# The out projection of an attention and mixture-of-experts kernel in three fp32r passes, with the low part of its input made on VectorE

## What is computed

```python
q1, k1, v1 = heads(ln(x) @ Wq1), heads(ln(x) @ Wk1), heads(ln(x) @ Wv1)
q2, k2, v2 = heads(ctx @ Wq2), heads(ctx @ Wk2), heads(ctx @ Wv2)
out1 = softmax(q2 @ k1.T * SCALE) @ v1
out2 = softmax(q1 @ k2.T * SCALE) @ v2
out = merge_heads(out1 * alpha + out2 * (1 - alpha))        # 256 x 512 for a sequence
x = x + out @ Wout + bout                                   # the out projection
h = ln(x)
scores = renormalised top 4 of softmax(h @ gate_w.T)
x = x + sum over experts of scores * (silu(h @ w1) * (h @ w3)) @ w2
```

## Time and profile before

| | us |
|---|---|
| median of 3 runs | 2166.13 |
| lowest, highest | 2165.26, 2168.65 |
| the profiled execution | 2171.79 |
| its span, first to last instruction | 2170.0 |

### The profile page before, as it was taken

One profiled execution on the slowest core, in us unless ns is written; L12 is line 12 of the kernel. 1 busy time (PEld: TensorE's weight loads), 2 busy tenths in 40 slices (PEclk: granted clock), 3 DMA queues, 4 the chain that ended last, 5 costly groups with the idle time before them and its releaser, 6 DMA issues.

```text
span 2170.0 us, 51710 instructions
## 1 busy us (share of the span) xinstructions
PE 1921.2 (89%) x15782; PEld 1684.2 (78%) x15783; DVE 1387.6 (64%) x3231; ACT 1235.5 (57%) x3605; POOL 1224.9 (56%) x1688
## 2 busy tenths in 40 slices
PE   6899999999999999999999999996898888888500
PEld 5788888888888888888888888885888888888500
DVE  4567666766667666677666776678554444444398
ACT  5666666666666666667666676663444444444300
POOL 3356666566665656666666666665455454554400
PEclk9999999999999999999999999998999999998855
DMA  4331111111111111101111101116664444444299
GB/s 131 114 96 44 44 46 61 39 44 42 48 61 39 44 40 50 51 34 39 39 42 51 39 34 44 39 61 188 192 215 143 143 143 140 140 143 139 109 412 360
DMA packets 158560, 210.80 MB, mean 97 GB/s; under 512 B 24224, under 2 KB 131376, under 8 KB 158512
## 3 DMA queue, kind: packets, MB, share of 16 engines
q1 hardware_dynamic: 123696, 129.95, 19.0%
q0 software_dynamic: 26112, 71.86, 9.2%
q10 hardware_dynamic: 8704, 8.39, 1.1%
HBM read 113.02 MB, written 97.12 MB: 97 GB/s over the span
## 4 chain that ended last, share of the span: by engine, by line
PE 66%; issue 8%; DVE 7%; ACT 5%; another core or an unknown queue 4%; DMA 4%; POOL 4%; SPq 0%; ACTq 0%; DVEq 0%; POOLq 0%
PE p_pt L1363 10%; PE p_s L1346 9%; PE p_av L1383 8%; PE p_s L1284 8%; PE p_gu L1567 6%; PE p_x L1284 4%; DVE z_ahead L1251 4%; PE p_s L1294 3%; PE p_x L1414 3%; ACT probs L705 3%; PE p_y L1588 3%; PE p_av L1284 2%; POOL x_rows L575 2%; POOL probs L583 2%
## 5 line engine op out<-in xcount | busy, mean ns | idle before, releaser
L583 POOL TENSOR_TENSOR probs<-probs,inv 128x256 f32<-128x256 f32 x1024 | 598.0, 615 | 407.6 <-DVE inv L968 406.6
L705 ACT ACTIVATE probs<-p_s,nmx 128x256 f32<-128x256 f32 x1024 | 474.5, 482 | 75.1 <-PE p_pt L1363 44.5
L961 DVE TENSOR_REDUCE nmx<-p_s 128x4 f32<-128x1024 f32 x256 | 312.0, 1219 | 122.1 <-PE p_s L1346 122.1
L575 POOL DMA_INDIRECT x_rows<-routed,slot_i x248 | 247.9, 1000 | 134.5 <-DVE target L953 70.2
L1363 PE MATMUL p_pt<-ident,probs 128*128 128x128 f32 x2048 | 292.6, 279 | 8.1 <-POOL probs L583 4.7
L1383 PE MATMUL p_av<-probsT,val 128*64 128x256 f32 x2048 | 258.9, 389 | 7.6 <-DVE probsT L856 4.5
L1363 PEld LDWEIGHTS p_pt<-ident,probs 128*128 128x128 f32 x2048 | 230.6, 142 | 41.1 <-issue 11.7
L693 ACT COPY probsT<-p_pt 128x512 f32<-128x512 f32 x256 | 151.5, 592 | 169.0 <-PE p_pt L1363 168.5
L1208 DVE TENSOR_TENSOR xgT_lo<-p_xt,xgT_hi 128x512 fp32r<-128x512 f32 x144 | 99.2, 689 | 205.5 <-ACT xgT_hi L813 155.2
L856 DVE COPY probsT<-p_pt 128x512 f32<-128x512 f32 x256 | 175.9, 687 | 70.7 <-PE p_pt L1363 36.7
L705 ACT ACTIVATION_READ_ACCUMULATOR probs<-p_s,nmx 128x1 f32 x1024 | 216.5, 211 | 0.0
(11 more groups left out here) (234 smaller groups left out, 5240.1 us busy)
## 6 DMA issues: line engine op xcount, KB each, us to landing
y_in<-y_rows SPq DMA_DIRECT2D x32, 1024.0 KB, 8.2
xg<-x_rows SPq DMA_DIRECT2D x72, 257.0 KB
xg_more<-x_rows SPq DMA_DIRECT2D x72, 257.0 KB
rows<-in_ctx_dram SPq DMA_DIRECT2D x32, 256.0 KB, 2.6
x_in<-in_x_dram SPq DMA_DIRECT2D x32, 256.0 KB, 2.8
mid_rows<-x_mid SPq DMA_DIRECT2D x32, 256.0 KB
x_rows<-bias SPq DMA_DIRECT2D x32, 256.0 KB, 3.2
z_ahead<-mid_rows SPq DMA_DIRECT2D x24, 256.0 KB
```

Of the source, the lines that this page charges most:

```text
L575: pool.indirect_dma_start(x_rows, bass.IndirectOffsetOnAxis(ap=slot_i[:, t, k:k + 1], axis=0), to_send[:, t, k, :], None).then_inc(last_se ...
L583: pool.tensor_tensor(pr[:, h, t, :], pr[:, h, t, :], rc[:, g:g + 1].to_broadcast([P, S]), ALU.mult).then_inc(normed_p, 1)
L705: act.activation(probs[u % 2][:, h, t, :], p_s[:, 2 * (u % 2) + h, t * S:(t + 1) * S], ACT.Exp, bias=nmx[u % 2][:, g:g + 1], accum_out=sum ...
L961: dve.tensor_reduce(nmx[i][:, :], p_s[:, 2 * i:2 * i + 2, :].rearrange("p h (t k) -> p (h t) k", t=ST), AX.X, ALU.max, negate=True).then_i ...
```

## The change

- `attnT` becomes two fp32r tiles, attnT_hi and attnT_lo. ACT writes the high part, as before from p_av, and DVE the low part: `attn_rest(b, p)`, p_av minus the high part, semaphore attn_lo. Every PE wait on attn_out becomes a wait on attn_lo.
- `wout` becomes two fp32r tiles. Wout is loaded as a seventh early piece, through a slot, converted by ACT and subtracted by DVE ahead of projection 8 of the first batch.
- Each matmul of the out projection becomes three, over `PASSES`.
- Room: a few tiles share memory in another way; of the 16 tiles for the experts' rows, 6 in place of 8 are loaded before the last scores are done.

```diff
@@ tiles
-            attnT = sb("attnT", [P, PAIRS, S], stack=a)
+            attnT = [sb(f"attnT_{part}", [P, PAIRS, S], F32R, a) for part in ("hi", "lo")]
-            wout = sb("wout", [P, PAIRS, D], stack=a)
+            wout = [sb(f"wout_{part}", [P, PAIRS, D], F32R, a) for part in ("hi", "lo")]
...
@@ loads
+        v = early_slots[len(early) % 4]
+        early.append((v, [(v.rearrange("p (c n) -> p c n", c=PAIRS), Wout.rearrange("(c p) n -> p c n", p=P))],
+                      flat(wout[0][:, :, :]), flat(wout[1][:, :, :]), 1.0))
+        EARLY = len(early)
...
-        EARLY_BEFORE = {0: (3,), 3: (4,), 8: (5,)}
+        EARLY_BEFORE = {0: (3,), 3: (4,), 8: (5, 6)}
...
-            sp.dma_start(wout[:, :, :], Wout.rearrange("(c p) n -> p c n", p=P)).then_inc(wout_in, 16)
...
-                if r == LOADS // 2:
+                if r == XG_ROWS:
                     sp.wait_ge(scores_done, STEPS * B)
@@ ACT
-                act.copy(attnT[:, p, :], p_av[:, 0:S]).then_inc(attn_out, 1)
+                act.copy(attnT[0][:, p, :], p_av[:, 0:S]).then_inc(attn_out, 1)
@@ DVE
+            def attn_rest(b, p):
+
+                dve.wait_ge(attn_out, PAIRS * b + p + 1)
+                dve.tensor_tensor(attnT[1][:, p, :], p_av[:, 0:S], attnT[0][:, p, :].bitcast(F32),
+                                  ALU.subtract).then_inc(attn_lo, 1)
...
                     row_max(b, 0)
                 if prev:
+                    attn_rest(pb, PAIRS - 2)
                     probsT_out(pb, STEPS - 2)
...
                     row_max(b, 2)
+                if prev and cur:
+                    attn_rest(pb, PAIRS - 1)
+                if cur:
                     probsT_out(b, 0)
...
                     if not cur:
-                        late_pieces(2, 6)
+                        late_pieces(2, 4)
+                        attn_rest(pb, PAIRS - 1)
+                        late_pieces(4, 6)
...
                 if cur:
+                    attn_rest(b, 0)
                     row_max(b, 4)
...
                 if cur:
+                    attn_rest(b, 1)
                     row_max(b, 6)
@@ PE (the same in project 7 and 10, attend 6, moe_rows_t and iteration)
-                pe.wait_ge(attn_out, PAIRS * (b + 1) - 1 + part)
+                pe.wait_ge(attn_lo, PAIRS * (b + 1) - 1 + part)
...
-                    pe.wait_ge(wout_in, 16)
+                    pe.wait_ge(early_lo, EARLY)
                 for t, c in OUT_PARTS[part]:
-                    mm = pe.matmul(p_x[:, t * D:(t + 1) * D], attnT[:, c, t * P:(t + 1) * P], wout[:, c, :],
-                                   start=(c == 0), stop=(c == PAIRS - 1))
+                    for i, (r, w) in enumerate(PASSES):
+                        mm = pe.matmul(p_x[:, t * D:(t + 1) * D], attnT[r][:, c, t * P:(t + 1) * P], wout[w][:, c, :],
+                                       start=(c == 0 and i == 0), stop=(c == PAIRS - 1 and i == 2))
```

More of the change, by code:

```diff
@@ L131, in xattn_moe_kernel @@
             rowsT = [[sb(f"rowsT{i}_{part}", [P, KT, S], F32R, a) for part in ("hi", "lo")] for i in range(2)]
+            with ExitStack() as planning_first:
+                first = lambda name, shape, dt=F32: sb(name, shape, dt, planning_first)
+                count_f = first("count_f", [P, E])
+                over_f = first("over_f", [P, E, MOST])
+                full = first("full", [P, E])
+                trin_f = first("trin_f", [P, E, E])
+                ends_f = first("ends_f", [P, E])
+                past_f = first("past_f", [P, FIRST, E])
+                texp_f = first("texp_f", [P, FIRST])
+                tstart_f = first("tstart_f", [P, FIRST])
+                trow_f = first("trow_f", [P, FIRST])
+                table_f = first("table_f", [P, 2, FIRST])
             gate_rows = sb("gate_rows", [E, D], stack=a)
@@ L204, in xattn_moe_kernel @@
                 table = plan("table", [P, 2, TC])
[L205 to L208, removed]
+            z_first = [sb(f"z_ahead{i}", [P, ST, D], stack=later) for i in range(9)]
+            sb("filler", [P, PAIRS * S * 8 + ST * INNER * 2 - (LOADS - XG_ROWS) * 2 * ROW - 9 * ST * D], stack=later)
+            xg = [sb(f"xg{i}", [P, 2, ROW], stack=later) for i in range(XG_ROWS)]
+            xg += [xg_more[:, i, :, :] for i in range(LOADS - XG_ROWS)]
             xgT = [[sb(f"xgT_hi{i}", [P, 2, KT, P], F32R, later), sb(f"xgT_lo{i}", [P, 2, KT, P], F32R, later)]
@@ L214, in xattn_moe_kernel @@
             y_out = [sb(f"y_out{i}", [P, 2, D], stack=later) for i in range(4)]
-            z_ahead = z_first + [sb(f"z_ahead{i}", [P, ST, D], stack=later) for i in range(11, Z_AHEAD)]
+            z_ahead = z_first + [sb(f"z_ahead{i}", [P, ST, D], stack=later) for i in range(9, Z_AHEAD)]
         assert 4 * TOP_K + B - Z_AHEAD <= (E * KT * 2 * I + E * D) // (ST * D)
@@ L269, in xattn_moe_kernel @@
             "pt_done", "pt_out_a", "pt_out_b", "av_done", "attn_out", "outp_done", "mid_set")
+        attn_lo = new("attn_lo")
         stats_set, mv_set, ve_set, rstd_set, ln1_set, ln2_set, x_res_set = new(
@@ L1307, in project @@
                 elif n == 7:
-                    wait(pe, attn_out, PAIRS * b - 2)
+                    wait(pe, attn_lo, PAIRS * b - 2)
                 elif n == 0:
@@ L1315, in project @@
                 elif n == 10:
-                    wait(pe, attn_out, PAIRS * b)
+                    wait(pe, attn_lo, PAIRS * b)
                 elif n == 8 and isinstance(b, int) and b == 0:
@@ L1375, in attend @@
                 if u == 6:
-                    pe.wait_ge(attn_out, PAIRS * b + 3)
+                    pe.wait_ge(attn_lo, PAIRS * b + 3)
                 elif u == 1:
@@ L1401, in moe_rows_t @@
                 if cur:
-                    pe.wait_ge(attn_out, PAIRS * (m + 1) + 1)
+                    pe.wait_ge(attn_lo, PAIRS * (m + 1) + 1)
                 transpose_rows(p_av, lambda t: rows_to_send(m)[:, t, 0, 0:D]).then_inc(moe_t, 1)
@@ L1459, in iteration @@
                     else:
-                        pe.wait_ge(attn_out, PAIRS * b - 2)
+                        pe.wait_ge(attn_lo, PAIRS * b - 2)
                     attend(pb, 4)
@@ L1515, in iteration @@
                     else:
-                        pe.wait_ge(attn_out, PAIRS * b + 1)
+                        pe.wait_ge(attn_lo, PAIRS * b + 1)
                     attend(b, 2)
```

26 lines of the change are left out of this document (9 added, 17 removed).

## The result

| | before | after | forecast |
|---|---|---|---|
| median, us | 2166.01 (4 runs) | 2191.65 (4 runs) | 2189.2 |
| lowest, highest | 2165.26, 2168.65 | 2188.18, 2193.99 | 2178 to 2206 |
| ratio | | 1.0114 [1.0096, 1.0131] | 1.0107 |
| profiled execution, span | 2171.79, 2170.0 | 2192.09, 2190.3 | 2194.9 for the execution |

The account below looks back on a forecast made before the run. PE was taken to bound the batch loop. Waits of 1.11 us less 0.40 of gaps gave 0.71 us a batch, 22.0 over 31, plus 1.1 at the start: +23.1 us, 2189.2 us, range 2178 to 2206.

Parts of the forecast that it names:

- PE's own work: Out projection: 24 fp32r passes 0.119 us apart replace 8 fp32 matmuls, saving 0.60 us a batch, 18.6 us over 31.
- a saving of 0.87 us: Out projection, per batch, if passes cost a quarter of fp32: 8 us less, 2181 us; rival, chance 0.08.
- The two waits: PE waits for DVE's pair 2 and 3 subtractions behind row_max: parts 0 and 1 end 0.54 and 0.57 us later.
- The wake-up of 0.13 us: Time from the subtraction's end to PE's start of each part; taken as the middle of 0 to 0.24 us.
- Pairs 0 and 1: Their DVE subtractions stand ahead of row_max 4 and 6, where DVE waits anyway; costed at nothing, at most 0.41 us each.
- The gaps: PE's idle time of 0.48 us a batch in two places; 0.40 us of it would absorb the waits.
- gap A: PE idle ahead of the attention of step 1, for DVE's copy of probsT; a quarter microsecond on average, taken as closed.
- gap S: PE idle ahead of scores 3, for ACT's exponentials; a quarter microsecond on average, a little over half taken as swallowed.
- Rival (1): Gaps don't close but move along, as late transposes hold back exponentials and these the scores: 35.5 us, 2202 us; chance 0.16.
- The ends: First batch: early Wout conversion and subtraction, 1.1 us later; last batch: nothing added, up to 2 us to the range.
- The sum: Whole kernel: 22.0 us over 31 batches plus 1.1 us at the start, +23.1 us, giving 2189.2 us; chance 0.56.
- Rival (3): Low part ready before PE asks in both parts, so only the saving is left: 2148.6 us; chance 0.05.

Follow-up runs that it names:

- waits_only: Changed kernel with the out projection back to 8 plain fp32 matmuls, low parts still made and waited for; ratio to before 1.0200.
- both_early: Changed kernel with DVE's subtractions of pairs 2 and 3 ahead of row_max 0 and row_max 2; ratio to before 1.0007, taken again on chip 3 1.0025.
- best: Changed kernel with both subtractions early, scores 2 ahead of scores 3, eighth send ahead of x_res, second early piece moved ahead of projection 9; ratio to before 0.9913.
- swap_send7: Changed kernel with both subtractions early, scores 2 ahead of scores 3 on PE and POOL's eighth send ahead of x_res; ratio to before 0.9855.
- the control: Kernel before, without the change, with scores 2 ahead of scores 3 and the eighth send ahead of x_res; ratio to before 0.9947, 2142.37 us.

## Why the prediction was right, point by point

**PE's own work.** Forecast 0.60 us a batch; measured 0.62 (waits_only against the changed kernel). The matmuls of the out projection are 0.11 to 0.12 us apart in the rows above, as I took from the earlier trace rows. The Trainium skill, FP8 and Floating Point Precision, section TensorE Precision Notes, counts four passes for true fp32. The estimate by that was a saving of 0.87 us, and the 0.62 us measured here do not bear it out.

**The two waits.** Part 0: stall forecast 0.69 us, net of what the matmuls save +0.54; measured 1.18 us from the transposes to part 0 against 0.49 before, 0.69, and +0.53 net. Part 1: forecast 0.86 and +0.57; measured 1.72 against 0.93 us, 0.79, and +0.51 net. The wake-up of 0.13 us was 0.13 and 0.06 us. (The rows' brackets say 0.53 and 0.63, since there the idle time begins at the modelled end of the transposes.) Both follow PE around, as said: all 28 batches carry them.

Pairs 0 and 1 were costed at nothing, and nobody but the out projection waits for line 968.

**The gaps.** Forecast: 0.40 of 0.48 us swallowed, gap A closed, gap S by a little over half. Measured: 0.35 us swallowed, and the other way round, gap S closed in full and gap A by half (0.25 to 0.14). The sum was right and its two terms were not, which is luck. Rival (1) rested on the late transposes holding back the exponentials one for one. The exponentials do wait for the transposes' semaphore, as the bracket of the second row below says, but that semaphore did not come later by as much as the transposes: in the kernel before, the exponentials started 1.76 us after POOL's third send in a row, in the changed kernel 1.79 us after it, and POOL's sends had not moved as far as PE. Before:

```profile
818.25 0.96 POOL L575 DMA_INDIRECT x_rows<-routed,slot_i  x1 [0.30 <-issue]
...
820.01 0.47 ACT L705 ACTIVATE probs<-p_s,nmx 128x256 f32<-128x256 f32 x1 [0.55 <-remote]
```

and after:

```profile
826.56 0.96 POOL L584 DMA_INDIRECT x_rows<-routed,slot_i  x1 [0.30 <-issue]
...
828.35 0.47 ACT L714 ACTIVATE probs<-p_s,nmx 128x256 f32<-128x256 f32 x1 [0.61 <-PE p_pt L1386]
```

From part 0's start (816.55; after: 825.54) the exponentials are 3.46 us away before and 2.81 us after. PE came later and they did not by as much. The delay of the semaphore fell from 1.81 to 1.29 us, under the 1.50 us at which gap S begins, and that is why it closed.

**The ends.** Forecast +1.1 us at the start: the first part 0 starts 2.13 us later (91.89 against 89.75), of which 0.52 is its own stall (1.01 us from the transposes against 0.49), so 1.6. At the last batch I had added nothing and kept up to 2 us for the range. x_mid, which started at 1493.46 us, now starts at 1517.29 us, 23.8 us later and so 1.8 us more than the last part 0, which moved from 1485.86 to 1507.91 us: the last subtraction waited 1.21 us for ACT and stood between late pieces.

```profile
1514.33 0.42 DVE L968 TENSOR_TENSOR attnT_lo<-p_av,attnT_hi 128x256 fp32r<-128x256 f32 x1 [1.21 <-ACT attnT_hi L706]
...
1517.29 0.69 DVE L1104 TENSOR_TENSOR x_mid<-p_x,x_res 128x512 f32<-128x512 f32 x1 [0.27 <-PE p_x L1438]
```

**The sum.** +23.1 us forecast; measured +23.8 at x_mid. The two profiled spans differ by 20.3 us only: from x_mid to the end it is 676.5 us before and 673.0 us after. The medians differ by 25.6 us. The 5.3 us between these two differences come from the profiled executions, that of before being 5.7 us above its median and that of after 0.4 us. Which part of the kernel varies from run to run, and whether the smaller number of rows loaded early has a share in the 3.5 us, stays open. The range was a little too narrow by its own terms: 2189.2 + 7 + 12.4 is 2208.6 and not 2206 us.

**Where it was wrong.** Rival (3) priced the kernel without waits at 2148.6 us, since "only the saving is left". That step, a microsecond of PE work that goes is one gained, failed. both_early is that kernel, and it ties with before. PE was busy 99.6% of the loop, and still the loop had two more limits within 0.5 us of it: POOL's eighth send behind x_res, and the exponentials behind the transposes' semaphore. Without waits the saving went into them: gap S grew from 0.24 to 0.55 us, gap A from 0.25 to 0.61 us. They showed in the kernel before as the two gaps of a quarter of a microsecond, and I had used these only as something that could be swallowed. A gap that is there in some batches meant here that another path is as long as PE's: it gives back what PE loses, and takes what PE wins.

## What to carry to other kernels

Where an engine that is busy all the time shows small gaps that come and go, another path is as long as its own: cap what a saving on it can bring, at nothing if need be, until that path is shorter too. Here three passes without any wait for them brought nothing on two chips. With one send and one pair of scores reordered the kernel was 18.1 us faster than before, 9.6 us of it beyond what the same reorderings brought alone. A value made on a second engine costs by its place in that engine's program, not by its length: the same 0.41 us subtraction cost 0.8 us of PE behind a row maximum and nothing ahead of it. And measure a change together with the version of before that has the same reorderings, or it is credited with what they bring.

## What the hardware showed that I had not expected

**The end of PE's transposes reaches the other engines late on some chips.** DVE's copy behind the last transposes of a batch started 3.57 us after part 0 in both_early on chip 1 and 3.48 us in best on chip 3, and 1.96 us in swap_send7 on chip 2, with PE's matmuls and POOL's sends at the same places. The time of PE's semaphore says the same. On chip 2 it changed 0.29 us after the start of the last transpose, in all four kernels and every batch. On chips 1 and 3 it came in nearly every batch of the loop 1.6 to 1.8 us after the start of POOL's third indirect send in a row (the fifth of a batch's eight), with the send anywhere from 0.71 us ahead of that transpose (waits_only) to 0.30 us behind it (both_early), and so 1.05 to 2.1 us after the transpose. In the kernel before it was 1.0 us after the send in some batches, in the control in most. In one batch in the middle of the loop the third send started 2.3 us after the transpose, in every kernel, and there the semaphore came 0.29 us after the transpose and gap S was nothing. Against it stand a few batches (one in waits_only, and some outside the hardware loop) with the send at its usual place and the semaphore at 0.29 us. That is a correlation. No run here moves these three sends away by themselves; that wasn't tried, and why one chip is free of it is open. The Trainium skill, Perfetto Trace Analysis, section Per-engine timelines, tells that a matmul's end in the profile is an estimate and that the semaphore update follows when PSUM has acknowledged that all bytes are written. The trace agrees that the update is an event of its own, 0.29 to 2.1 us behind the start of a transpose; the rows of PE don't show such a delay, and only those of the waiting engines do.

**Chips differ in one stage.** The attention loop ran at the same pace on chips 2 and 3 where the gaps allowed it (44.03 us a batch in swap_send7; 44.34 less its gap S of 0.33 in best); the stage behind it was 115 us shorter on chip 2 (554.1 against 669.4 us). The cause is open.
